# Experts by sorted token tiles, moved by indirect DMA, in place of a dense pass over all experts

## The reference, cut to what matters

```python
scores = softmax(xn @ gate_w.T)            # 8 experts
w, chosen = top_k(scores, 2);  w = w / sum(w)
routed = sum over the two chosen e of  w_e * (silu(xn @ wg[e]) * (xn @ wu[e])) @ wd[e]     # 176 hidden each
shared = (silu(xn @ swg) * (xn @ swu)) @ swd                                              # 352 hidden
g = silu(routed + shared)
```

## Time and profile before

| | us |
|---|---|
| median of 3 runs | 1713.17 (1711.78 to 1713.24) |
| span of the profiled execution (the page gives no other time for it) | 1708.8 |
| PE, DVE, ACT, POOL busy | 1513.5, 1319.0, 1217.6, 1099.4 |
| `front` / `window_attention` / `experts` / the rest | 30.8 / 230.9 / 298.1 / 1149.0 |

### The profile page before, as it was taken

One profiled execution on the slowest core, in us unless ns is written; L12 is line 12 of the kernel. 1 busy time (PEld: TensorE's weight loads), 2 busy tenths in 40 slices (PEclk: granted clock), 3 DMA queues, 4 the chain that ended last, 5 costly groups with the idle time before them and its releaser, 6 DMA issues. The chain is left out here.

```text
span 1708.8 us, 44008 instructions
## 1 busy us (share of the span) xinstructions
PE 1513.5 (89%) x16988; PEld 1164.6 (68%) x16988; DVE 1319.0 (77%) x2187; ACT 1217.6 (71%) x2065; POOL 1099.4 (64%) x661
## 2 busy tenths in 40 slices
PE   5899996999999499999999578899999999999885
PEld 4677774677776266666666467777777777777774
DVE  5899974555655699999997788887888888888753
ACT  2677774545445488888888378888888888888873
POOL 1777752555555388888887477776676777667614
PEclk8899998999999699999999689999999999999997
DMA  5000000000000500000000001111111110111113
GB/s 174 2 3 3 3 3 15 15 8 7 7 7 1 185 2 2 14 2 14 2 14 11 13 22 31 27 26 27 27 27 27 27 26 22 26 27 27 27 27 105
DMA packets 56837, 44.12 MB, mean 26 GB/s; under 512 B 28152, under 2 KB 47900, under 8 KB 56388
## 3 DMA queue, kind: packets, MB, share of 16 engines
q1 hardware_dynamic: 56644, 41.45, 9.1%
HBM read 17.75 MB, written 4.23 MB: 13 GB/s over the span
## 5 line engine op out<-in xcount | busy, mean ns | idle before, releaser
L831 POOL TENSOR_TENSOR a_prob<-a_prob,a_top 128x1024 f32<-128x1024 f32 x128 | 239.8, 1895 | 48.2 <-DVE a_top L1023 48.2
L1237 POOL TENSOR_TENSOR e_hh<-e_h,e_hh 128x512 fp32r<-128x512 f32 x112 | 144.8, 1293 | 146.6 <-ACT e_hh L1221 145.2
L1506 POOL TENSOR_TENSOR i_qk<-i_qk,i_rt 128x1024 f32<-128x1024 f32 x64 | 152.0, 2375 | 38.1 <-DVE i_rt L1955 33.3
L1516 POOL TENSOR_TENSOR i_qk<-i_qk,i_rn 128x1024 f32<-128x1024 f32 x64 | 122.5, 1915 | 80.5 <-DVE i_rn L1934 80.5
L1019 DVE TENSOR_TENSOR a_prob<-ps,a_table 128x1024 f32<-128x1024 f32 x128 | 149.7, 1211 | 23.4 <-PE ps L899 21.3
L1811 ACT ACTIVATE i_prob<-i_prob,i_top 128x128 f32<-128x128 f32 x512 | 156.4, 391 | 15.7 <-DVE i_top L1943 13.8
L977 ACT ACTIVATE a_probT<-ps 128x1024 f32<-128x1024 f32 x128 | 131.3, 1026 | 44.5 <-PE ps L907 44.5
L1258 DVE TENSOR_TENSOR e_h<-ps,e_sg 128x512 f32<-128x512 f32 x112 | 77.3, 690 | 104.3 <-PE ps L1120 90.4
L907 PEld LDWEIGHTS ps<-ident,a_prob 128*128 128x128 f32 x1024 | 113.2, 141 | 64.2 <-ACT a_probT L977 50.3
L1503 POOL TENSOR_TENSOR i_qk<-i_raw,i_rot 128x1024 f32<-128x1024 f32 x59 | 140.3, 2378 | 24.1 <-issue 24.1
L1208 ACT ACTIVATE e_sg<-ps 128x512 f32<-128x512 f32 x112 | 67.0, 598 | 123.2 <-PE ps L1120 122.4
(11 more groups left out here) (305 smaller groups left out, 4369.3 us busy)
## 6 DMA issues: line engine op xcount, KB each, us to landing
i_V<-i_V SPq DMA_DIRECT2D x96, 130.0 KB, 2.3
a_table<-skew_scratch SPq DMA_DIRECT2D x2, 2048.0 KB, 12.4
X<-in_L_attn_x SPq DMA_DIRECT2D x4, 512.0 KB, 6.1
a_table<-in_c_l_table SPq DMA_DIRECT2D x1, 2048.0 KB, 8.3
e_xs<-Y SPq DMA_DIRECT2D x8, 256.0 KB, 2.3
i_ms<-Y SPq DMA_DIRECT2D x16, 128.0 KB, 2.4
i_ms<-Y SPq DMA_DIRECT2D x16, 112.0 KB, 2.4
out_dram<-X SPq DMA_DIRECT2D x7, 256.0 KB, 2.3
```

Source lines behind the costliest of these rows:

```text
L831: nc.gpsimd.tensor_tensor(s, s, top[:, slot].unsqueeze(2).broadcast_to([P, HG, KW]), ALU.subtract).then_inc(shifted, 1)
L1237: nc.gpsimd.tensor_tensor(hh[0:n, slot(b, parity), 1, :], h[0:n, slot(b, parity), :], hh[0:n, slot(b, parity), 0, :].bitcast(F32), ALU.sub ...
L1506: nc.gpsimd.tensor_tensor(s, s, rt[:], ALU.add).then_inc(rotated, 1)
L1516: nc.gpsimd.tensor_tensor(flat, flat, rn[:, T // TPB % 2, T % TPB].unsqueeze(2).broadcast_to([P, 2 * FH, FD]), ALU.mult).then_inc(qk_done, 1)
```

## The change

The routing now gives each token and each of its two experts a place in a list of slots of 128 rows, each slot of one expert. Tokens are sorted in two groups of 16 tiles; each group has 40 slots, 80 in all, of which some rows stay empty. The places are computed on the chip: a matmul with a triangular matrix gives each row's rank within its tile (a new PE job at step 7 of attention), and DVE sums over tiles and experts (`choose_experts`, at steps 4, 8, 12 and 16). POOL writes each tile's 128 rows of `Y` to their slots in DRAM by two indirect DMAs, the first group's 32 in attention, one behind each unit from unit 24 on, the second group's at the start of `experts`. So that empty rows hold zeros, `front` clears the slots' 5.2 MB first. In `experts` a pair of slots is loaded, transposed, multiplied with its expert's weights, whose offset PE loads into a register, and written back; POOL gathers the two results of each token by 64 indirect DMAs. The shared expert stays dense, in 8 rounds, and DVE adds the two weighted results. Routed products are plain float32; those of the shared gate and up stay split.

```diff
+GROUPS = 2
+GT = NT // GROUPS
+GROUP_SLOTS = 2 * ((2 * GT + NE) // 2)
+SLOTS = GROUPS * GROUP_SLOTS
...
+def scatter_rows(nc, Y, plan, n, c):
+
+    where = bass.IndirectOffsetOnAxis(ap=plan["at"][:, n, c:c + 1], axis=0)
+    nc.gpsimd.indirect_dma_start(out=plan["xp"][n // GT], out_offset=where, in_=Y[:, n, :], in_offset=None).then_inc(plan["scattered"][n // GT], 16)
...
 in front, SP and POOL:
+            sp.wait_ge(nothing_set, 1)
+            for a in range(0, SLOTS, 8):
+                g, b = divmod(a, GROUP_SLOTS)
+                sp.dma_start(plan["xp"][g][b * P:(b + 8) * P, :].rearrange("(c p) e -> p c e", p=P), nothing[:]).then_inc(plan["cleared"], 16)
...
             sp.wait_ge(rel_out, 16)
+            sp.wait_ge(plan["cleared"], 16 * SLOTS // 8)
...
+            nc.gpsimd.memset(nothing[:], 0.0).then_inc(nothing_set, 1)
...
 in window_attention:
+        RANK = 7
+        CHOICE = (4, 8, 12, 16)
+        SCATTER = 24
+        EACH = 1 if GROUPS > 1 else 2
...
                 shift(n)
-                i, r = divmod(n + 2, U)
+                if n == SCATTER:
+                    pool.wait_ge(plan["placed"], 1)
+                for m in range((n - SCATTER) * EACH, (n - SCATTER + 1) * EACH):
+                    if 0 <= m < 2 * GT:
+                        scatter_rows(nc, Y, plan, *divmod(m, 2))
...
-                if step >= 4 and step % 8 == 4 and step // 8 < 5:
-                    between(dve, 1 + step // 8)
+                if step in CHOICE:
+                    choose_experts(nc, dve, 1 + CHOICE.index(step), route, plan)
...
 in experts:
+    XB, YB = 4, 4
+    LAG = 7
...
+        def _(sp):
+            for signal in used:
+                sp.sem_clear(signal)
+            for j in range(PAIRS + LAG):
+                if is_pair(j):
+                    if j % GROUP_PAIRS == 0:
+                        sp.wait_ge(scattered[j // GROUP_PAIRS], 16 * 2 * GT)
+                    after(sp, xs_T, j - XB + 1)
+                    sp.dma_start(xs[:, j % XB], rows(xp, j)).then_inc(xs_loaded[j % XB], 16)
+                if is_pair(j - LAG):
+                    d = j - LAG
+                    sp.wait_ge(ys_sb, d + 1)
+                    sp.dma_start(rows(yp, d), ys[:, d % YB]).then_inc(ys_out[d % YB], 16)
...
+        def _(pool):
+            for g in range(1, GROUPS):
+                for n in range(g * GT, (g + 1) * GT):
+                    for v in range(2):
+                        scatter_rows(nc, Y, plan, n, v)
+            for n in range(NT):
+                if n % GT == 0:
+                    results_stored(pool, (n // GT + 1) * GROUP_PAIRS)
+                for v in range(2):
+                    where = bass.IndirectOffsetOnAxis(ap=plan["at"][:, n, v:v + 1], axis=0)
+                    nc.gpsimd.indirect_dma_start(out=yg[:, n, v, :], out_offset=None, in_=yp[n // GT], in_offset=where).then_inc(gathered[n // 4], 16)
...
+            def place_weights(j):
+                for k in range(2):
+                    t = 2 * j + k
+                    chosen[t] = nc.tensor.value_load(weights_at[0:1, t:t + 1], min_val=0, max_val=(NE - 1) * EW)
...
+                    last = nc.tensor.matmul(ps[:, 2 * (j % 2) + k, 0:2 * INTER], xsT[:, j % 2, k * P:(k + 1) * P],
+                                            flat[:, bass.ds(chosen[2 * j + k], 2 * INTER)], start=True, stop=True)
...
+            for step in STEPS:
+                if is_pair(step + 1):
+                    place_weights(step + 1)
+                if is_pair(step):
+                    first_products(step)
+                if is_pair(step - 1):
+                    slot_hidden(step - 1)
+                if is_pair(step + 2):
+                    slot_tokens(step + 2)
+                if is_pair(step - 2):
+                    slot_results(step - 2)
+            for i in range(ROUNDS + 1):
+                if i == 0:
+                    tokens(0)
+                if i < ROUNDS:
+                    shared_products(i)
+                if i + 1 < ROUNDS:
+                    tokens(i + 1)
+                if i:
+                    shared_results(i - 1)
```

More of the change, by code:

```diff
@@ L233, in router_buffers @@
 def router_buffers(nc, ctx):
     sb = lambda n, s, d=F32: ctx.enter_context(nc.sbuf_tensor("r_" + n, s, d))
[L236 to L244, removed]
+    wide = {n: sb(n, [P, NT, NE]) for n in ("lg", "rest", "first", "second", "chosen", "place")}
@@ new lines, in choose_experts @@
+        dve.drain()
+    elif part == 3:
+        for k in range(3):
+            src, dst, reach = slot_scan[:, k % 2], slot_scan[:, 1 - k % 2], 1 << k
+            nc.vector.tensor_tensor(dst[:, :, EPAD:EPAD + NE], src[:, :, EPAD:EPAD + NE], src[:, :, EPAD - reach:EPAD + NE - reach], ALU.add)
+            dve.drain()
+        begin = slot_scan[:, 1, :, EPAD - 1:EPAD + NE - 1]
+        for g in range(GROUPS):
+            nc.vector.scalar_tensor_tensor(grouped(place)[:, g], begin[:, g].unsqueeze(1).broadcast_to([P, GT, NE]), float(P), grouped(place)[:, g], ALU.mult, ALU.add)
+        dve.drain()
+        for c, one in enumerate((first, second)):
+            nc.vector.tensor_tensor(rest[:], place[:], one[:], ALU.mult)
+            dve.drain()
+            nc.vector.tensor_reduce(where[:, :, c], rest[:], AX.X, ALU.add)
+            dve.drain()
+        nc.vector.tensor_copy(plan["at"][:], where[:]).then_inc(plan["placed"], 1)
+    else:
+        begin = slot_scan[0:1, 1, :, EPAD - 1:EPAD + NE - 1]
+        full = [1, GROUPS, GROUP_SLOTS, NE]
+        numbers = slots[:, :].rearrange("p (g t) -> p g t", g=GROUPS)
+        nc.vector.tensor_tensor(listing[:], numbers.unsqueeze(3).broadcast_to(full), begin.unsqueeze(2).broadcast_to(full), ALU.is_ge)
+        nc.vector.tensor_tensor(st[:, :], best[:, 0, :], best[:, 1, :], ALU.add)
+        dve.drain()
+        nc.vector.tensor_reduce(numbers, listing[:], AX.X, ALU.add)
@@ L284, in choose_experts, with front @@
         dve.drain()
[L285 to L299, removed]
+def front(nc, t, ps, X, Y, ident, wts, plan, skew, attn, route):
+    full = SHARED // P
@@ L1286, in _, with slot_products, keep_slot_rest @@
[L1286 to L1289 removed]
+            def slot_products(j):
+                dve.wait_ge(silu_sb, j + 1)
+                after(dve, h_T, j - 1)
+                b = 2 * (j % 2)
+                nc.vector.tensor_tensor(hs[:, j % 2], ps[:, b:b + 2, INTER:2 * INTER], sg[:, j % 2], ALU.mult).then_inc(h_sb, 1)
+            def keep_slot_rest(j):
+                dve.wait_ge(h_T, j + 1)
+                after(dve, ys_ps, j - 1)
+                nc.vector.tensor_copy(hrT[:, j % 2, :], ps[0:REST, 5, 0:2 * P]).then_inc(h2_sb, 1)
@@ L1291, in inner_layers @@
+            for i in range(ROUNDS + 2):
+                if i < ROUNDS:
+                    for s in range(NC):
+                        products(i, s)
+                if i + 1 < ROUNDS:
+                    low_tokens(i + 1)
+                if 1 <= i <= ROUNDS:
+                    mix(i - 1)
+                if i >= 2:
+                    new_rows(i - 2)
+def inner_layers(nc, t, ps, ident, X, Y, kept, out, weights, stored):
     KW = 2 * WIN
```

517 lines of the change are left out of this document (284 added, 233 removed).

## The result

The changed kernel takes 1672.3 us (median of 4 runs, 1670.6 to 1673.7) against 1713.2: a ratio of 0.9761, 95% interval 0.9742 to 0.9779. The prediction, 1658 in a range of 1618 to 1712, has the direction and holds the time in a range 94 us wide; the point is 14 us too low.

The account below looks back on a forecast made before the run. TensorE's columns in the experts' dense pass were taken as the bound. Experts -86, front +13, choosing +5 and GpSimd's transfers +13 sum to -55 us, from 1713 to 1658, range 1618 to 1712.

Parts of the forecast that it names:

- The dense pass as the bound, and its end: Experts' block: TensorE's columns in the dense pass set its time; replacing it takes 212 against 298.1 us, 86 less.
- The expert pairs: Experts' block: 40 pairs of slots, bound by PE at 3.05 us each, take 122 us.
- Registers: Experts' pairs: loading two slot offsets into PE registers leaves 0.2 us per pair uncovered, 8 us in all.
- rival B: Experts' pairs: register loads stand in the open, 1.2 us per pair, 40 us more, 1698 us; chance 0.20.
- The shared part: Experts' block, after the pairs: 8 rounds of 8.3 us, 66 us, plus a tail of 5.5.
- The front: Front: ten clears of 512 KB on SP's queue, whose landing its end awaits, lengthen it by 13 us.
- GpSimd's price: Attention: 32 indirect transfers on GpSimd delay the units' subtractions, 13 us; those in the experts are hidden.
- c: GpSimd's time per indirect transfer, in attention and experts: taken as 1.3 us, bounded by 0.61 and 2.38.
- the estimate with 1.0: Attention: at 1.0 us per GpSimd transfer, 4 of the 13 us would remain, time 1649 us.
- Choosing: Attention: added routing operations on VectorE exceed its slack of 0.36 us per unit, costing 5 us.
- A: Rival, attention and experts: GpSimd's transfers at 2.6 us each make the kernel slower, 1737 us; chance 0.11.
- C: Rival: all hidden, c at most 0.89, no register time or routing stall, clears at 437 GB/s; about 1627 us; chance 0.20.

Follow-up runs that it names:

- Full rows: Changed kernel with each slot's second down product contracting over 128 rows instead of 48, zeros beside the real ones; 1640.2 us.

## Why the prediction was right, and where it was not

- **The dense pass as the bound, and its end.** Right: the block fell by 69.8 us (86 predicted), and PE has no gap in the steady pairs.
- **The expert pairs,** 122 + 8 us predicted, 40 x 3.51 = 140 measured. The term that failed is "four down products of 128 columns, 8 x 0.125 = 1.00": it measured 1.57, 23 us over 40 pairs. The row of its price had products of one form only; the second product of each slot contracts over 48 rows, and the step did not ask whether the trace of before shows such a change. It has one, in attention: behind sixteen instructions over 32 rows (L601) the weight loads of L583 begin only with their first product, at 150.17 us and after 0.81 us without a load, where those of L609 begin at 150.92, 0.22 us ahead of theirs. Full rows brought the eight to 0.89. Against it, first products and transposes were 0.11 per pair too dear, 4 us, and the registers' 8 were not spent.
- **Registers (rival B).** Fell: no gap at the pairs' first products, and constant addresses changed nothing. The 600 ns for a register load in the Trainium skill, "DMA: Bandwidth & Descriptors", section on latency and other measured facts, show nowhere on PE here: without 78 of the 80 loads a pair still takes 3.51 us.
- **The shared part,** 66 + 5.5 predicted, 442.5 to 519.9 = 77.4 measured. The rounds were shorter than the 8.3 (seven from the first sums at 460.6 to the last at 512.8, 7.45 each) and the tail longer (7.1 for 5.5), but above all the step left out the start: 18.1 us from the first transposes at 442.5 to the first sums at 460.6, in which two rounds of products come first and PE's granted clock was 0.50, then 0.67, to 450 us.
- **The front,** 13 predicted, 13.8 measured, with SP last. The size was right, and so was the price: the clears held SP for 19.0 us, where the prediction had 18 for 5.24 MB at 290 GB/s. The prediction named two waits, for the clears' landing and for the bias table behind them on SP's queue, and priced the first; the one that ended last was the second. With the wait for the landing gone and the issues left in the front, it still ended at 42.7.
- **GpSimd's price,** c = 1.3 predicted: 1.2 in attention, 1.26 back to back in the experts (0.96 and 0.30 of issue). The 1 us of descriptor writing in the Trainium skill, "DMA: Bandwidth & Descriptors", section on latency and other measured facts, fits the 0.94 to 1.01 that nearly all records show; the issue of 0.17 to 0.30 comes on top, so that the estimate with 1.0 was too low. The units with scatters had no gaps on POOL, as forecast, at 3.55 us in place of 3.65. From the eighth key mask to the end attention took 143.1 us against 135.8, so 7.3 where 13 stood.
- **Choosing,** 5 predicted. From the first to the eighth key mask 98.2 us against 89.5 before, 8.7. The step was priced with each operation's length alone; a part of it is waiting for POOL: a cast at 117.24 us lasts 1.24 and ends with the subtraction of 116.36 to 118.43. How much of the 8.7 this makes is not shown. That the two terms come near in sum, 18 predicted and 16.1 measured, is luck: one was 6 too high, the other 4 too low.
- **Rivals A and C.** A would have needed c above 2.35, and the gathers end at 485.5, ahead of the last sums at 513. C failed at c, which is above 0.89, at the clears and at the routing; only its free registers came true.

By the sum: front +0.8, attention -1.9, experts +16.2 against the forecast, -0.3 in the rest: 14.8 on the span, and 12.6 on the profiled execution's time, which lies 2.0 us over its span where 4.4 was carried over. That the time lies in the range says little by itself; the parts say where the prediction held.

## What to carry to other kernels

A price read from a row holds for its form: where a new loop alternates products over different numbers of contraction rows, look for a row with that very change (128 and 48 rows cost here, 128 and 96 did not), or pad the short one with zeros, which here gave some 30 us for no more products. A wait that is moved frees an engine only when the issues move too. Operations put into VectorE's slack took their own length only where GpSimd had gaps; look at the neighbour's order of time before choosing the place.

## What was not expected of the hardware

- A change between float32 products over 128 and over 48 contraction rows costs 0.15 to 0.17 us on PE; a change between 128 and 96 contraction rows, or between transposes of 128 and of 48 output rows, none.
- Ten issues on SP of 512 KB each, with rows of 512 bytes, hold SP for 15 to 19 us: the first on empty DMA engines takes 0.39 us, the later ones up to 2.1.
- VectorE's cast of 80 numbers took 4.27 us beside a busy GpSimd. To move the casts to ScalarE was not tried.
- The granted clock of the front fell at different moments from profile to profile of nearly the same code, from 18 to 30 us, and moved the front's end by some 6 us where nothing else held it. What decides the moment stays open.
